# Attention sums placed behind the first two FFN residuals, a three-instruction norm chain on GpSimd, and weight splits shared by three engines

## What is computed

```python
for l in range(3):
    si = x @ attn_w[l, :d]
    sj = x @ attn_w[l, d:]
    scores = si[:, :, None] + sj[:, None, :] + attn_b[l]
    scores = jnp.where(scores >= 0, scores, 0.2 * scores)
    scores = jnp.where(mask, scores, -jnp.inf)
    attn = jax.nn.softmax(scores, axis=-1)
    agg = jnp.einsum('bij,bjd->bid', attn, x)
    h = layernorm(x + agg, g1[l], beta1[l])
    ff = jax.nn.gelu(h @ W1[l] + b1[l], approximate=False) @ W2[l] + b2[l]
    x = layernorm(h + ff, g2[l], beta2[l])
```

## Time and profile before

| | |
|---|---|
| median of 3 runs | 1864.64 us (1861.49 to 1866.35) |
| the profiled execution, its own time | 1871.55 us |
| its span in the trace | 1869.6 us |
| PE busy | 1670.7 us, 89% |
| PE weight loads busy | 1475.7 us, 79% |
| DVE busy | 1379.5 us, 74% |
| POOL busy | 1269.8 us, 68% |
| ACT busy | 1206.6 us, 65% |
| granted TensorE clock, mean | 0.959 |

### The profile page before, as it was taken

One profiled execution on the slowest core, in us unless ns is written; L12 is line 12 of the kernel. 1 busy time (PEld: TensorE's weight loads), 2 busy tenths in 40 slices (PEclk: granted clock), 3 DMA queues, 4 the chain that ended last, 5 costly groups with the idle time before them and its releaser, 6 DMA issues.

```text
span 1869.6 us, 40745 instructions
## 1 busy us (share of the span) xinstructions
PE 1670.7 (89%) x12032; PEld 1475.7 (79%) x12032; DVE 1379.5 (74%) x5414; ACT 1206.6 (65%) x2814; POOL 1269.8 (68%) x2260
## 2 busy tenths in 40 slices
PE   5999999974999999998899999999988999999995
PEld 4777877863888888888788888888877888887894
DVE  2888888887776777667766776677676887777873
ACT  3888888873665666656555666666656666666662
POOL 3255555533676766767566866766767999998996
PEclk8999999995999999999989999999999999999997
DMA  6222232332211212212131211212211222122111
GB/s 183 63 89 81 84 90 90 90 97 85 74 49 52 67 34 67 61 40 68 34 97 49 67 46 55 67 34 67 67 34 57 68 68 90 59 76 73 66 42 45
DMA packets 152115, 127.39 MB, mean 68 GB/s; under 512 B 16512, under 2 KB 145024, under 8 KB 152064
## 3 DMA queue, kind: packets, MB, share of 16 engines
q1 hardware_dynamic: 145024, 124.30, 21.6%
q10 hardware_dynamic: 7040, 2.51, 0.5%
HBM read 89.04 MB, written 37.75 MB: 68 GB/s over the span
## 4 chain that ended last, share of the span: by engine, by line
PE 28%; POOL 17%; DVE 9%; issue 8%; DMA 7%; SPq 4%; ACT 3%; POOLq 0%; ACTq 0%; DVEq 0%
PE ps L834 13%; PE ps L45 10%; DMA ab<-in_L_gnn_attn_b 7%; POOL xo L772 5%; POOL gnn_norm L766 4%; POOL gnn_norm L156 4%; DVE gnn_junk L940 3%; PE ps L821 3%; POOL inv L151 2%; DVE gnn_st L1007 2%; DVE gnn_res L1003 2%; PE ps L807 2%; SPq L124 1%; SPq L126 1%; SPq L689 1%
## 5 line engine op out<-in xcount | busy, mean ns | idle before, releaser
L834 PE MATMUL ps<-gnn_w_hi,gnn_g_hi 128*128 128x256 f32 x1536 | 446.6, 291 | 70.7 <-DVE gnn_res L1003 70.5
L834 PE MATMUL ps<-gnn_w_lo,gnn_g_hi 128*128 128x256 f32 x1536 | 435.6, 284 | 0.0
L834 PE MATMUL ps<-gnn_w_hi,gnn_g_lo 128*128 128x256 f32 x1536 | 435.3, 283 | 0.0
L143 POOL TENSOR_TENSOR fence_pool<-half_neg 128x1 f32<-128x1 f32 x346 | 65.8, 199 | 501.4 <-DVE gnn_mv L1101 235.3
L917 ACT ACTIVATE gnn_g_hi<-ps,b_cols 128x512 fp32r<-128x512 f32 x384 | 264.6, 689 | 211.8 <-PE ps L45 211.7
L1011 DVE TENSOR_TENSOR gnn_g_lo<-ps,gnn_g_hi 128x512 fp32r<-128x512 f32 x384 | 263.0, 685 | 161.7 <-ACT ps L918 161.6
L834 PEld LDWEIGHTS ps<-gnn_w_hi,gnn_g_hi 128*128 128x128 f32 x1536 | 296.0, 193 | 81.3 <-DVE gnn_res L1003 78.8
L45 PE MATMUL ps<-gnn_hT_hi,gnn_w_hi 128*128 128x512 f32 x768 | 341.1, 444 | 3.9 <-DVE gnn_g_lo L1011 3.9
L45 PE MATMUL ps<-gnn_hT_lo,gnn_w_hi 128*128 128x512 f32 x768 | 305.6, 398 | 0.0
L45 PE MATMUL ps<-gnn_hT_hi,gnn_w_lo 128*128 128x512 f32 x768 | 305.5, 398 | 0.0
L940 DVE CUSTOM_DVE_ANT_0 gnn_junk<-x,aw 128x256 f32<-128x256 f32 x384 | 213.1, 600 | 120.6 <-DMA ab<-in_L_gnn_attn_b 120.1
(11 more groups left out here) (120 smaller groups left out, 3882.5 us busy)
## 6 DMA issues: line engine op xcount, KB each, us to landing
hist<-xo SPq DMA_DIRECT2D x48, 512.0 KB, 3.3
x<-hist SPq DMA_DIRECT2D x48, 512.0 KB, 4.2
gmask<-mask_hist SPq DMA_DIRECT2D x48, 256.0 KB, 4.2
aw<-in_L_gnn_attn_w SPq DMA_DIRECT2D x48, 256.0 KB, 4.1
att_xq<-in_x SPq DMA_DIRECT2D x16, 512.0 KB, 4.6
att_xl<-in_x SPq DMA_DIRECT2D x16, 512.0 KB, 3.6
gnn_fin<-hist SPq DMA_DIRECT2D x16, 512.0 KB, 3.9
out<-gnn_fin SPq DMA_DIRECT2D x16, 512.0 KB, 3.0
```

Of the source, the lines that this page charges most:

```text
L834: mm = e.matmul(FF2[j % 2], g[a][:, m, j * N:(j + 1) * N], V[b][:, m, :], start=(n == 0), stop=(n == len(terms) - 1))
```

## The change

It has three parts.

1. In DVE's tail, the sums for graphs 0 and 1 of step t+3 move from ahead of `residual2(0)` and `residual2(1)` to behind both (and behind `final_statistics` in the last layer), ahead of `residual2(2)`; the sums for graphs 2 and 3 move from ahead of `residual2(2)` to behind `hT_lo`.
2. `layernorm_on_pool` computes rstd with one addition of a constant tile `eps` and one power, and the wide instructions do (y - mean) * rstd from the statistics directly, in place of y * rstd + (-mean * rstd). Three small instructions (addition, power, fence) are left of five. The callers wait for their input by a plain wait and not by a fence.
3. The weight splits: the high part of W1 is copied by ACT at a layer's end (`split_w1_hi`, between `exps` and `hT_hi`), the low part stays on DVE in two pieces; the high part of W2 stays on DVE in `new_layer`, its low part is halved between DVE and POOL. POOL's half (`split_w2_lo`, four instructions of 128x256) stands ahead of `ln_ffn` in the last step of a layer and waits for the high part that DVE makes in `new_layer`. One pair of semaphores for each of W1 and W2 replaces the shared pair; PE and SP wait for them. ACT and POOL now also have the last pair of a layer written out (`peel_layer_end`).

```diff
         def layernorm_on_pool(e, chain, n0, stats, inv, y, dest, done=None):
-            e.tensor_scalar(inv[:, 0, :], stats[:, :, 1], EPS, None, ALU.add).then_inc(chain, 1)
-            e.tensor_scalar(inv[:, 1, :], stats[:, :, 0], -1.0, None, ALU.mult).then_inc(chain, 1)
+            e.tensor_tensor(inv[:, 0, :], stats[:, :, 1], eps[:], ALU.add).then_inc(chain, 1)
             e.wait_ge(chain, n0 + 1)
-            e.tensor_tensor(inv[:, 2, :], inv[:, 0, :], half_neg[:], ALU.pow).then_inc(chain, 1)
-            e.wait_ge(chain, n0 + 3)
-            e.tensor_tensor(inv[:, 3, :], inv[:, 1, :], inv[:, 2, :], ALU.mult).then_inc(chain, 1)
-            hold_pool(e, chain, n0 + 4)
+            e.tensor_tensor(inv[:, 1, :], inv[:, 0, :], half_neg[:], ALU.pow).then_inc(chain, 1)
+            hold_pool(e, chain, n0 + 2)
             for j in range(GROUP):
-                last = e.tensor_scalar(dest[:, j, :], y[:, j, 0:D], inv[:, 2, j:j + 1], inv[:, 3, j:j + 1],
-                                       ALU.mult, ALU.add)
+                last = e.tensor_scalar(dest[:, j, :], y[:, j, 0:D], stats[:, j, 0:1], inv[:, 1, j:j + 1],
+                                       ALU.subtract, ALU.mult)
...
                 def ln_ffn(t, par, half, last_layer):
-                    hold_pool(e, mv2_out, t + 1)
-                    layernorm_on_pool(e, ln2, 5 * t, mv2, inv, y2, norm, norm2_out)
+                    e.wait_ge(mv2_out, t + 1)
+                    layernorm_on_pool(e, ln2, 3 * t, mv2, inv, y2, norm, norm2_out)
...
+                def split_w2_lo(l):
+                    e.wait_ge(w2_hi_set, l + 1)
+                    for m in range(FT // 2):
+                        ins = e.tensor_tensor(V[1][:, m, :], w2_raw[:, m, :], V[0][:, m, :].bitcast(F32), ALU.subtract)
+                    ins.then_inc(w2_split, 1)
...
+                    if layer_end:
+                        split_w2_lo(layer_of(2 * q + par + 1))
                     ln_ffn(2 * q + par, par, q, final or isinstance(q, int))
...
+                def split_w1_hi(l):
+                    e.wait_ge(w_ld, 32 * (l + 1))
+                    for k in range(KT):
+                        e.copy(W[0][:, k, :], w1_raw[:, k, :]).then_inc(w1_hi_set, 1)
...
                     if more >= 2:
                         exps(t + 2)
+                    if layer_end:
+                        split_w1_hi(layer_of(t + 1))
                     if more >= 1:
                         hT_hi(t + 1)
...
-                    if more >= 3:
-                        attention_sums(t3, p3, h3, 0)
                     residual2(t, par, 0)
                     if more >= 2:
                         probs_max(t2)
                     if final:
                         final_sum(q, par)
-                    if layer_end:
-                        split_w1(layer_of(t1), 0)
-                    if more >= 3:
-                        attention_sums(t3, p3, h3, 1)
                     residual2(t, par, 1)
                     if layer_end:
-                        split_w1(layer_of(t1), 1)
+                        split_w1_lo(layer_of(t1), 0)
                     if final:
                         final_statistics(q, par)
                     if more >= 3:
+                        attention_sums(t3, p3, h3, 0)
+                        attention_sums(t3, p3, h3, 1)
+                    residual2(t, par, 2)
+                    if layer_end:
+                        split_w1_lo(layer_of(t1), 1)
+                    if more >= 1:
+                        hT_lo(t1)
+                    if more >= 3:
                         attention_sums(t3, p3, h3, 2)
                         attention_sums(t3, p3, h3, 3)
-                    residual2(t, par, 2)
-                    if layer_end:
-                        split_w1(layer_of(t1), 2)
-                        split_w1(layer_of(t1), 3)
-                    if more >= 1:
-                        hT_lo(t1)
                     for j in range(3):
                         stats2(t, j)
                     residual2(t, par, 3)
...
                     e.wait_ge(w_ld, 32 * (l + 1))
-                    e.tensor_copy(V[0][:], w2_raw[:]).then_inc(w_hi_set, 1)
-                    e.wait_ge(w_hi_set, 3 * l + 3)
-                    e.tensor_tensor(V[1][:], w2_raw[:], V[0][:].bitcast(F32), ALU.subtract).then_inc(w_split, 1)
+                    e.tensor_copy(V[0][:], w2_raw[:]).then_inc(w2_hi_set, 1)
+                    e.wait_ge(w2_hi_set, l + 1)
+                    e.tensor_tensor(V[1][:, FT // 2:FT, :], w2_raw[:, FT // 2:FT, :], V[0][:, FT // 2:FT, :].bitcast(F32),
+                                    ALU.subtract).then_inc(w2_split, 1)
```

More of the change, by code:

```diff
@@ L95, in gnn_kernel @@
         half_neg = sb("half_neg", [P, GROUP])
+        eps = sb("eps", [P, GROUP])
         w1_raw = sb("w1_raw", [P, KT, F])
@@ L707, in _ @@
                 with e.Fori(0, L - 1) as l:
-                    e.wait_ge(w_split, 2 * (l + 1))
+                    e.wait_ge(w1_split, 2 * (l + 1))
+                    e.wait_ge(w2_split, 2 * (l + 1))
                     load_layer_weights(e, l + 1)
@@ L752, in ln_attention @@
                     ins.then_inc(ln1, 1)
-                    e.wait_ge(ln1, 5 * t1 + 5)
+                    e.wait_ge(ln1, 3 * t1 + 3)
                     for j in range(GROUP):
@@ L787, in body @@
                         final_norm(t1, p1)
+                    if layer_end:
+                        split_w2_lo(layer_of(2 * q + par + 1))
                     ln_ffn(2 * q + par, par, q, final or isinstance(q, int))
                 ln_attention(0, 0)
-                steps(e, body, peel_last_layer=True)
+                split_w2_lo(0)
+                steps(e, body, peel_layer_end=True, peel_last_layer=True)
                 final_norm(T - 1, 1)
@@ L924, in body @@
                             gelu_table(1)
+                split_w1_hi(0)
                 exps(0)
@@ L929, in _ @@
                 hT_hi(0)
-                steps(e, body)
+                steps(e, body, peel_layer_end=True)
             @block.vector
@@ L1036, in final_statistics, with split_w1_lo @@
                     ins.then_inc(mv3_out, 1)
-                def split_w1(l, n):
-                    k = n % 2
-                    if n < 2:
-                        if n == 0:
-                            e.wait_ge(w_ld, 32 * (l + 1))
-                        e.tensor_copy(W[0][:, k, :], w1_raw[:, k, :]).then_inc(w_hi_set, 1)
-                    else:
-                        e.wait_ge(w_hi_set, 3 * l + k + 1)
-                        ins = e.tensor_tensor(W[1][:, k, :], w1_raw[:, k, :], W[0][:, k, :].bitcast(F32), ALU.subtract)
-                        if n == 3:
-                            ins.then_inc(w_split, 1)
+                def split_w1_lo(l, k):
+                    e.wait_ge(w1_hi_set, KT * l + k + 1)
+                    e.tensor_tensor(W[1][:, k, :], w1_raw[:, k, :], W[0][:, k, :].bitcast(F32), ALU.subtract).then_inc(w1_split, 1)
                 def body(q, par, more, layer_end, final):
```

33 lines of the change are left out of this document (16 added, 17 removed).

## The result

The changed kernel is slower: 1956.55 us median (four runs, 1955.76 to 1958.24), against 1863.07 (1861.02 to 1866.35) for the kernel before on the same chip. The ratio is 1.0496, with a 95% interval of 1.0480 to 1.0513. The forecast was 1762 us, with a range of 1741 to 1812. The profiled execution took 1958.24 us, its span is 1956.1 and its mean granted clock 0.939.

What follows compares the result with a forecast made beforehand. The norm-store-load-sums ring, not PE, bounds layers 0 and 1; DVE's queue bounds layer 2. Gains of 105.5 us less 3 given back, 102.5, take 1871.6 to 1769.1; 6.9 lower for the median gives 1762, range 1741 to 1812.

Steps and rivals of the forecast that it cites:

- given back: Whole kernel: 3 us taken off the gain for two more engines whose last pair of a layer is written out.
- The ring and what is late next: Layers 0 and 1: the loop through norm, store, loads and sums is covered; PE bounds next, 26.2 us a step.
- the 0.7: GpSimd's small norm chain: 0.7 us saved per normalization, 2.36 to 1.7; in layers 0 and 1 worth nothing beyond covering the loads.
- second margin: Layers 0 and 1: another 0.7 us to spare at `hT_lo`, besides 0.3 us where the sums ask for the loads.
- Layer 2: Last layer: VectorE's queue is the bound; moved sums save 0.95 us a step, 11.4 us in all, bounds 8 and 20.
- The layer starts: Around the layer changes, with shared weight splits: 6.7 us gained in bodies 15 and 16, 8.4 in 31 and 32.
- The first stage: Ahead of the layers: GpSimd waits for VectorE there, so the shorter norm gains nothing.
- The end: Behind the last matmul: three normalizations on the path, each 0.7 us shorter, gain 2.1 us.
- Rival A: Layers 0 and 1: stalls shrink but the clock still falls every second step, 25 us less gain, 1787 us; chance 0.17.
- B: All eight sums slowed to 0.87 us by contention with GpSimd, nothing gained in layer 2, 1807 us; chance 0.13.
- C: Layers 0 and 1: the ring closes through `hT_lo`, 29.8 us a step, slower, 1872 us; chance 0.04.
- D: The load stall isn't removed, as loads come later by as much as was moved; about 1860 us; chance 0.06.

Runs made afterwards that it cites:

- e8: The changed kernel with the wide GpSimd instruction adding the mean instead of subtracting it, which computes another function: 1762.53 us, ratio 0.9463.
- e3: The kernel before with 20 spare GpSimd instructions of eleven forms between the first stage and the layers, results unread: 1864.32 us in one run.
- e1: The changed kernel with the norm helper of before put back, leaving the moved sums and the weight splits: 1791.42 us, ratio 0.9618.
- e4: The kernel before with only the order of the sums changed: 1787.68 us, ratio 0.9587.
- e9: The kernel before with only a new norm: negated mean from a small instruction, wide add-multiply, sums not moved: 1829.39 us, ratio 0.9805.
- e7: The kernel before with the moved sums and the norm that adds the negated mean, without the weight splits: 1762.56 us, ratio 0.9456.
- e11: The kernel with moved sums and negated-mean norm, no splits, given the long norm helper of before in the first stage alone: 1752.96 us, ratio 0.9403.

## Why the prediction was wrong

**The step that failed** is one sentence of part 2: "The wide instructions keep form and count (subtract, multiply instead of multiply, add)." They keep shape, type, count and instruction name, and I priced them by these, at nothing. The trace of before had no row for a subtract-multiply on POOL. The nearest rows should have given a lower and an upper bound for it; the sentence gave none, no rival carried it, and so neither the range nor the 0.04 for slower held it. Measured, it is 0.67 us for each of 512 instructions, and 194 us in the kernel's time (after against e8). The Trainium skill (GPSIMD Engine Reference, section 3.1, "Elementwise — side-by-side cycle accounting") gives costs per element that depend on the number of inputs and of operations in the loop, and none by operation; the rows of e3 differ by a factor of 2.2 at the same count.

**The other steps**, term by term. Gains in us against before, from the starts of the bodies; a minus is a loss. e8 is after without the failed step. The two sums differ by 0.1 from the spans, by rounding.

| stretch | predicted | after | e8 |
|---|---|---|---|
| up to body 1 | 0 | -1.9 | -6.5 |
| bodies 1 to 14 | 43.3 | -1.3 | 47.6 |
| 15 and 16 | 6.7 | -1.3 | 6.3 |
| 17 to 30 | 33.6 | -10.3 | 37.1 |
| 31 and 32 | 8.4 | -3.1 | 6.5 |
| 33 to 44 | 11.4 | -49.6 | 17.2 |
| 45 | 0 | -5.1 | 0.0 |
| behind the start of 46 | 2.1 | -14.0 | 1.7 |
| given back | -3.0 | | |
| sum | 102.5 | -86.6 | 109.9 |

- The ring and what is late next: right. PE is the bound, 362.52/14 = 25.89 us a step in e8, predicted 26.2 with a floor of 25.87. The 0.3 for jitter wasn't needed. DVE's wait for the loads is 15.3 us ("under 15"), 8.4 of it in one place.
- "If the 0.7 weren't there, the landing would come ... still inside the second margin": half right. e1 lacks the 0.7 and takes 26.44 a step in layer 0 (370.2/14), with 45.2 us of load waits in 30 places. The small chain is worth 0.5 us a step, some 14 us over both layers, where the prediction gave it nothing of its own. Both its size (0.8, predicted 0.7) and the narrow margin of 0.3 us were in the text; the step didn't add them up.
- Layer 2: the term was too small, and its reason incomplete. "The chain shows DVE, so I give POOL nothing more." e4 and e1 (moved sums, long norm) take 28.4 a step and e9 (short norm, sums not moved) 28.3, all close to 28.56 before; with both a step takes 27.1 (e8) and 27.4 (e7). So DVE's queue and POOL's must both get shorter. That they bound the step together is read from these times; the waits of a step weren't followed. POOL was busy 146.90 of 160 us in before, and that row should have stood in the argument.
- The layer starts: the total is right (12.8 of 15.1), the cause isn't. e7, with no change to the splits, takes 62.1 us for bodies 15 and 16 and 57.5 for 31 and 32, less than e8's 64.9 and 58.1. The moved sums bring the gain: e4 has nothing else and takes 62.95 and 59.37 for 71.2 and 64.6. POOL's half of W2 puts `xo` 3.6 us later at the start of layer 1; counted from the start of body 31 it is 1.0 at that of layer 2. The prediction had named that wait, and body 16 takes 37.09 us in e8 for its 37.8. What it lacked was the same step with the splits left alone: 33.11 in e7.
- The first stage, "POOL waits for DVE: nothing": wrong by 6.5 us. e11 shows that the shorter norm does it, most likely by moving POOL's next work onto DVE's. After itself shows only 1.9; its norm is longer than the old one.
- The end: 1.7 for 2.1.
- Rival A (the clock still falls) didn't happen: 4 dips in e8 for 22. Nor did B, C and D as priced. The time of e8, 1762.53, is the forecast's 1762, but partly by chance: the sum was 10.9 us short in the steps and layer starts, gave back 3 for the written-out pairs, a term that no run shows on its own, and left out the 6.5 of the first stage, 7.4 short in all. And the profiled execution of before lies 6.9 us above its median, which the forecast took off, while e8's (1761.94) lies at its median.

What the marks in the last part tell, read in after: the chain measures 1.56 (right), PE's wait for `gnn_res` is gone (right), the period isn't under 27 (wrong), the loads are waited for as before (wrong), and the clock still dips in layers 0 and 1 (32 stretches at half clock in all the layers, 22 before; wrong). PE doesn't wait for `hT_lo` in most steps, but for POOL's norm of step t+1, which no mark named. A mark on the wide instruction was missing.

## What to carry to other kernels

An instruction that keeps its name, shape and type but gets another operation is a new instruction: price it by a row of its own, or keep both bounds and a rival for it. For fp32 tiles like these, write the norm on GpSimd as (y + (-mean)) * rstd or y * rstd + b and not with a subtraction in the wide instruction, and spend a small instruction on the sign. When a helper is shared between stages, ask in each of them what the engine does next and what that will now meet: here the best kernel (e11) uses the short norm in the layers and the long one in the first stage.

## What was not expected of the hardware

- GpSimd's tensor_scalar on 128x256 fp32: with values from SBUF 0.55 us for multiply-add, add-multiply and multiply-multiply, 1.21 with a subtraction in either place, 0.92 for one operation alone, be it subtract or multiply. Why isn't known; no run here looks inside.
- Somewhat shorter stalls can bring nearly all of the clock back: a median of 1.11 us in place of 1.83, and 4 dips in place of 22. The gain of e9 (38 us by the medians) was expected at 16 to 28 from the shorter norm alone. In before the clock fell behind some stalls of 1.83 us and not behind some of 2.24; why isn't known.
- Shortening an engine's work can cost time, by what its next instructions then meet: the long norm in the first stage beats the short one by 9.6 us (e11 against e7).
